# A Mamba round with eight states scaled by ScalarE and folded by accumulating DMAs, and softplus sums moved to accumulating DMAs

## The reference, cut to what matters

```python
ssm = xv @ W_x
dt_raw, Bp, Cp = ssm[..., :8], ssm[..., 8:24], ssm[..., 24:]
delta = softplus(dt_raw @ W_dt + b_dt)
dA = exp(delta[..., None] * A)
dBx = delta[..., None] * Bp[:, :, None, :] * xv[..., None]
h = associative_scan(dA, dBx)          # h[l] = dA[l] * h[l-1] + dBx[l]
y = einsum('bldn,bln->bld', h, Cp) + xv * D
s = y @ W_out
x = x + s * silu(ffn(xn))
```

## Time and profile before

| What | us |
|---|---|
| median of three runs | 855.91 |
| the profiled execution, its own time | 857.77 |
| its span in the trace | 856.0 |
| Mamba rounds, first scan to the end | 406.4 to 856 |
| one round, start of `du` to start of the next | 54.7 to 54.9; 59.75 for the one that begins at 564.96 |
| busy in the span: PE, DVE, ACT, POOL | 680, 673, 485, 502 |

### The profile page before, as it was taken

One profiled execution on the slowest core, in us unless ns is written; L12 is line 12 of the kernel. 1 busy time (PEld: TensorE's weight loads), 2 busy tenths in 40 slices (PEclk: granted clock), 3 DMA queues, 4 the chain that ended last, 5 costly groups with the idle time before them and its releaser, 6 DMA issues. The chain is left out here.

```text
span 856.0 us, 13812 instructions
## 1 busy us (share of the span) xinstructions
PE 679.6 (79%) x4000; PEld 502.5 (59%) x4000; DVE 672.5 (79%) x1203; ACT 484.5 (57%) x946; POOL 501.5 (59%) x289
## 2 busy tenths in 40 slices
PE   1948999997999600376779889898898998989673
PEld 1925555655555400233567777676777876778573
DVE  5856777876656468602799999988999999999994
ACT  1725666565444223245685866946858668586461
POOL 1016510000000177007689999999899999999993
PEclk9968999999999855589899999999999999999998
DMA  8501100010222111022311420413203213142000
...
DMA packets 41608, 55.90 MB, mean 65 GB/s; under 512 B 6601, under 2 KB 31697, under 8 KB 41553
## 3 DMA queue, kind: packets, MB, share of 16 engines
q1 hardware_dynamic: 37776, 50.48, 18.2%
...
## 5 line engine op out<-in xcount | busy, mean ns | idle before, releaser
L1575 DVE TENSOR_TENSOR_SCAN xnT_all<-psum,nfT_all 128x1024 f32<-128x1024 f32 x128 | 285.6, 2273 | 7.9 <-ACT psum L1425 5.2
L1313 PEld LDWEIGHTS psum<-W_out,xnT_all 128*128 128x128 f32 x2048 | 244.1, 197 | 40.0 <-issue 38.0
L1313 PE MATMUL psum<-W_out,xnT_all 128*128 128x128 f32 x2048 | 246.5, 280 | 17.2 <-DVE acc L1591 17.2
L1425 ACT ACTIVATE psum<-delta,A 128x511 f32<-128x511 f32 x256 | 163.2, 678 | 40.7 <-DVE xnT_all L1575 39.9
L1293 POOL TENSOR_TENSOR nfT_all<-nf_all,du 128x1024 f32<-128x1024 f32 x64 | 149.8, 2368 | 7.8 <-DVE xnT_all L1575 7.8
L1293 POOL TENSOR_TENSOR nfT_all<-attn_all,du 128x1024 f32<-128x1024 f32 x64 | 149.3, 2359 | 2.5 <-DVE xnT_all L1575 1.2
L950 POOL COPY pos_w<-pos 128x4 uint32 x8 | 1.8, 222 | 182.8 <-issue 182.8
L1591 DVE SCALAR_TENSOR_TENSOR acc<-psum,Cc,acc 128x128 f32<-128x128 f32 x352 | 96.7, 342 | 7.8 <-PE psum L1313 7.8
L551 POOL DMA_INDIRECT xs_dram<-nf_all,pos x32 | 32.3, 1008 | 66.7 <-issue 55.9
L1313 PE MATMUL psum<-vo_all,wgu 128*128 128x512 f32 (+1 forms) x96 | 49.6, 642 | 26.5 <-DVE hff L1611 24.9
L1313 PE MATMUL psum<-vo_all,W_taps 128*128 (+4 forms) x128 | 60.5, 621 | 1.7 <-DVE psum L1558 1.7
...
## 6 DMA issues: line engine op xcount, KB each, us to landing
attn_all<-bt_dram SPq DMA_DIRECT2D x32, 512.0 KB, 5.4
nf_all<-bt_dram SPq DMA_DIRECT2D x32, 512.0 KB, 3.6
...
```

Source lines behind the costliest of these rows:

```text
L1313: return nc.tensor.matmul(o, l, r, start=start, stop=stop)
L1425: ins = nc.scalar.activation(dA[:, i % RA, k, 1:L], delta[:, p, h, 1:L], ACT.Exp, scale=A[:, h, 2 * q + k:2 * q + k + 1])
L1575: nc.vector.tensor_tensor_scan(hring[:, i % R, :, :].rearrange("p n l -> p (n l)"), dA[:, i % RA, :, :].rearrange("p n l -> p (n l)"), dbx ...
```

## The change

- `ON_ACT` becomes all eight odd states. ACT scales them into eight buffers of `ts`, one in each step: state 2q-1 in steps 1 to 7, state 15 in step 0 of the next round. DVE adds only the eight even states.
- The eight buffers are summed in four folds, written as DMAs that accumulate into their destination (`fold`, issued by POOL): `ts[2:4] += ts[0:2]` in step 7, then, in the next round, `ts[4:6] += ts[2:4]` in step 1, `ts[6:8] += ts[4:6]` in step 3 and `ts[7] += ts[6]` in step 4. The first three move 512 KB, the last 256 KB. Each waits for the fold before it. In the closing round the last three folds are additions on POOL.
- The three softplus sums become accumulating DMAs of 512 KB issued by POOL (`add_to`): `delta += rl`, `e1 += ab`, `delta += e1`. ACT now writes the log straight into `delta`. The third waits until the first two have landed, and `du` and the decays wait until the third has landed.
- `output` moves from step 3 to step 5, behind the issue of `delta += rl`.
- `fa` is gone: `ffn_hidden` works in place in `hff`.

The diff, cut to its core:

```diff
--- before.py
+++ after.py
@@ -1104,7 +1104,7 @@
             NP = NS // 2
             R = 4
             RA = 2
-            ON_ACT = (5, 7, 9, 15)
+            ON_ACT = tuple(range(1, NS, 2))
             ON_DVE = tuple(n for n in range(NS) if n not in ON_ACT)
 
             Bbc = attn_all[:, :, :].rearrange("p j d -> p (j d)").rearrange("p (n l) -> p n l", l=L)
...
-            accP = sb6("accP", [P, TPB, D])
...
+            s_sp = sem("p6_softplus_summed")
+            s_ts = sem("p6_scaled_states_summed")
+            s_last = sem("p6_last_scaled_states_summed")
...
@@ -1216,21 +1216,30 @@
                     def w(n, c):
                         pool.wait_ge(S[n], at(b + 1, n, c))
 
-                    def sum_scaled(c, i):
-
-                        pool.wait_ge(S["ts"], at(c, "ts", i + 1))
-                        pool.wait_ge(S["accP"], at(c, "accP", i if i > 1 else 0))
-                        if i == 1:
-                            pool.wait_ge(S["og"], at(c - 1, "og", 1))
-                        nc.gpsimd.tensor_tensor(accP[:, :, :], ts[:, 0, :, :] if i == 1 else accP[:, :, :],
-                                                ts[:, i, :, :], ALU.add).then_inc(S["accP"], 2 if i == 1 else 1)
+                    def fold(c, k):
+
+                        lo, mid, hi = ((0, 2, 4), (2, 4, 6), (4, 6, 8), (6, 7, 8))[k]
+                        pool.wait_ge(S["ts"], at(c, "ts", hi))
+                        if not scan and k > 1:
+                            pool.wait_ge(s_last, k - 1)
+                        elif k or end:
+                            pool.wait_ge(s_ts, c * 64 + k * 16)
+                        alone(pool)
+                        if scan:
+                            pool.dma_start(ts[:, mid:hi, :, :], ts[:, lo:mid, :, :], accum_op=ALU.add).then_inc(s_ts, 16)
+                        else:
+                            nc.gpsimd.tensor_tensor(ts[:, mid:hi, :, :], ts[:, mid:hi, :, :], ts[:, lo:mid, :, :], ALU.add)\
+                                .then_inc(s_last, 1)
 
                     def output():
 
                         pool.wait_ge(S["acc"], at(b - 1, "acc", len(ON_DVE) * TPB))
-                        pool.wait_ge(S["accP"], at(b - 1, "accP", len(ON_ACT)))
+                        if scan:
+                            pool.wait_ge(s_ts, b * 64)
+                        else:
+                            pool.wait_ge(s_last, 3)
                         pool.wait_ge(s_o, b * 16)
-                        nc.gpsimd.tensor_tensor(ow[:, :, :], acc[:, 1 - p, :, :], accP[:, :, :], ALU.add)\
+                        nc.gpsimd.tensor_tensor(ow[:, :, :], acc[:, 1 - p, :, :], ts[:, 7, :, :], ALU.add)\
                             .then_inc(S["os"], 1)
                         pool.wait_ge(S["os"], at(b - 1, "os", 1))
                         pool.wait_ge(S["G1"], at(b - 1, "G1", 1))
@@ -1241,30 +1250,28 @@
                         nc.gpsimd.tensor_tensor(ow[:, :, :], ow[:, :, :], x_all[:, ds((b - 1) * TPB, TPB), :], ALU.add)\
                             .then_inc(S["ow"], 1)
 
+                    def add_to(total, part):
+                        pool.dma_start(total, part, accum_op=ALU.add).then_inc(s_sp, 16)
+
                     def softplus_high():
-
                         w("lg", 1)
                         w("rl", KH)
-                        w("delta", 0)
                         alone(pool)
-                        nc.gpsimd.tensor_tensor(lg[:, :, :], lg[:, :, :], rl[:, :, :], ALU.add).then_inc(S["sp"], 1)
+                        add_to(delta[:, 1 - p, :, :], rl[:, :, :])
 
                     def softplus_low():
                         w("e1", 1)
-                        nc.gpsimd.tensor_tensor(e1[:, :, :], ab[:, :, :], e1[:, :, :], ALU.add)\
-                            .then_inc(S["corr"], 1)
+                        alone(pool)
+                        add_to(e1[:, :, :], ab[:, :, :])
 
                     def deltas():
-                        w("sp", 1)
-                        w("corr", 1)
-                        pool.wait_ge(S["dA"], at(b, "dA", 0))
-                        pool.wait_ge(S["du"], at(b, "du", 0))
-                        nc.gpsimd.tensor_tensor(delta[:, 1 - p, :, :], e1[:, :, :], lg[:, :, :], ALU.add)\
-                            .then_inc(S["delta"], 1)
+                        pool.wait_ge(s_sp, (b + 1) * 48 + 32)
+                        alone(pool)
+                        add_to(delta[:, 1 - p, :, :], e1[:, :, :])
 
                     def drives():
 
-                        w("delta", 1)
+                        pool.wait_ge(s_sp, (b + 2) * 48)
                         w("xv", KH)
                         pool.wait_ge(S["dbx"], at(b, "dbx", 0))
                         nc.gpsimd.tensor_tensor(du[:, 1 - p, :, :], delta[:, 1 - p, :, :], xv[:, :, :], ALU.mult)\
@@ -1273,19 +1280,19 @@
                     if scan:
                         pool.wait_ge(S["du"], at(b, "du", 1))
                         for q in range(NP):
-                            if q == 1 and end:
-                                sum_scaled(b - 1, 2)
-                            if q == 3 and end:
-                                sum_scaled(b - 1, 3)
-                                output()
-                            if q == 5 and prep:
-                                softplus_high()
+                            if q in (1, 3, 4) and end:
+                                fold(b - 1, (1, 3, 4).index(q) + 1)
+                            if q == 5:
+                                if prep:
+                                    softplus_high()
+                                if end:
+                                    output()
                             if q == 6 and prep:
                                 softplus_low()
                             if q == 7:
                                 if prep:
                                     deltas()
-                                sum_scaled(b, 1)
+                                fold(b, 0)
                             pool.wait_ge(s_bld[q], (b + 1) * 16)
                             for h in range(KH):
                                 i = 2 * q + h
@@ -1301,8 +1308,8 @@
                         deltas()
                         drives()
                     elif end:
-                        sum_scaled(b - 1, 2)
-                        sum_scaled(b - 1, 3)
+                        for k in (1, 2, 3):
+                            fold(b - 1, k)
                         output()
 
                 rounds(pool, round_)
@@ -1417,7 +1424,8 @@
                 def decays(b, p, q):
 
                     if q == 0:
-                        act.wait_ge(S["delta"], at(b, "delta", 1))
+                        act.wait_ge(s_sp, (b + 1) * 48)
+                        alone(act)
                     for h in range(KH):
                         i = 2 * q + h
                         act.wait_ge(S["scan"], at(b, "scan", i + 1 - RA))
@@ -1436,12 +1444,16 @@
                     nc.scalar.activation(bank[bM[h]], bank[bM[h]], ACT.Identity, bias=convb[:, h:h + 1])\
                         .then_inc(S["yh"], 1)
 
-                def scale_state(c, p, i):
+                def scale_state(c, p, i, again):
 
                     n = ON_ACT[i]
                     act.wait_ge(S["G"], at(c, "G", n + 1))
                     act.wait_ge(S["C"], at(c, "C", 1))
-                    act.wait_ge(S["accP"], at(c, "accP", max(i, 1) + 1 - len(ON_ACT)))
+                    if i == 7:
+                        act.wait_ge(S["os"], at(c - 1, "os", 1))
+                    elif again:
+                        act.wait_ge(s_ts, (c - 1) * 64 + (16, 16, 32, 32, 48, 48, 64)[i])
+                        alone(act)
                     for j in range(TPB):
                         ins = nc.scalar.activation(ts[:, i, j, :], bank[Gb[n % 2]][:, j * P:(j + 1) * P], ACT.Copy,
                                                    scale=Cc[:, p, j, n:n + 1])
@@ -1474,9 +1486,9 @@
 
                     def abs_relu(h):
                         w("dt_ps", h + 1)
-                        w("corr", 0)
-                        w("lg", 0)
-                        w("delta", 0)
+                        if scan:
+                            act.wait_ge(s_sp, (b + 1) * 48)
+                            alone(act)
                         nc.scalar.activation(ab[:, h, :], bank[bM[h]], ACT.Abs, bias=b_dt[:, h:h + 1])
                         nc.scalar.activation(rl[:, h, :], bank[bM[h]], ACT.Relu, bias=b_dt[:, h:h + 1])\
                             .then_inc(S["rl"], 1)
@@ -1487,13 +1499,13 @@
 
                     def ln_one_plus():
                         w("ey", 1)
-                        w("delta", 0)
-                        nc.scalar.activation(lg[:, :, :], ab[:, :, :], ACT.Ln, bias=1.0).then_inc(S["lg"], 1)
+                        act.wait_ge(S["du"], at(b, "du", 0))
+                        act.wait_ge(S["dA"], at(b, "dA", 0))
```

(8 more changed lines are left out.)

12 lines of the change are left out of this document (5 added, 7 removed).

## The result

The changed kernel takes **875.12 us** (median of four runs, 871.63 to 875.43) against 856.41 for the kernel before beside it (855.45 to 860.3): ratio 1.020, 95% interval 1.016 to 1.024. Forecast were 852.1, range 843 to 874. The sign was wrong, and the time lies 1.1 us above the range. The profiled execution has a span of 873.6 (own time 875.43) where before it was 856.0.

A forecast was written before the change was run, and what follows sets the result against it. The prediction took a loop through PE, ACT and DVE as the bound: seven rounds at −0.4, back edge −3.0, startup +1.0, round 7 −1.4 and closing +2.4 sum to −3.8, from 855.9 to 852.1 us, range 843 to 874.

The forecast's parts named there:

- The loop PE-ACT-DVE sets the pace: Round's loop through PE, ACT and DVE: 30.0 us of unchanged PE work plus the way back; gains 0.4, to 54.4.
- Busy times: Each engine's work per round: DVE falls to 49.3 us, ACT rises to 43.8, POOL needs 52.6.
- Issues, 1.26 (0.96 to 1.74): POOL's time to issue one DMA, seven added a round: 1.26 us, taken from indirect DMAs.
- issues as the bound: Rival: at 1.74 us an issue POOL needs 56.0 a round and sets the pace, total 866; chance 0.13.
- Landings, 4.2 from the end of the issue: Accumulating DMAs of 512 KB land 4.2 us after their issue ends, bounds 2.7 and 7.0; at 4.2 nothing stalls.
- landings as the bound: Rival: waits along `e1 += ab`, `delta += e1`, `du` in steps 6 and 7 decide from 6.4 us; chance 0.22.
- ACT in steps 6 and 7: "nothing": ACT's added scalings there, 1.05 us each, fall into its waits for PE and cost nothing.
- `output` behind the log: POOL, step 5: waits some 3 us for the log, then 27.7 us to the first dbx, leaving 2.2 slack.
- Startup +1.0: Before the first scan: two issues and two uncovered landings replace two sums, costing 1.0 us.
- Back edge −3.0: Between rounds 2 and 3, where DVE jumps back: PE's wait and slow `ssm` mostly go, saving 3.0 us, bounds 0 and 4.2.
- Round 7, −1.4: Round that prepares nothing: DVE saves 3 us by step 7, but POOL's input comes later, so 1.4 us is gained.
- Closing +2.4: Closing round: one addition behind the last `ts` becomes two, costing 2.4 us.

The follow-up runs named there:

- e6: Changed kernel with SP's store behind the B loads, ACT's next-round decays before step 7's scaling, and in-round B loads filling one partition, not 128: 856.06 us, ratio 0.999.
- e11: Changed kernel with SP's store behind the B loads, ACT's next-round decays before step 7's scaling, and B loads spread one at a time: 860.64 us, ratio 1.003.
- e13: e12 with ACT's scalings of steps 1 and 2 put back where the changed kernel has them: 852.51 us, ratio 0.992.
- e8: Changed kernel with the three softplus sums as additions on POOL again, folds still accumulating DMAs: 867.9 us, ratio 1.012.
- e10: e8 with ACT writing the next round's first decays ahead of the scaling of state 13 in step 7: 863.44 us, ratio 1.004.
- e7: Changed kernel with its accumulating DMAs made plain copies of the same size, the sums left out: 862.31 us, ratio 1.006.
- e2: Changed kernel with ACT writing the next round's step 0 decays ahead of the scaling of state 13 in step 7: 875.41 us, ratio 1.020.
- e4: Kernel before, with its loads of B held back and issued in a bundle, no accumulating DMAs: 858.43 us, ratio 0.999.
- e9: Changed kernel with four states on ACT, their additions on POOL and ACT's order as before; softplus sums still accumulating DMAs: 866.01 us, ratio 1.009.
- e12: Changed kernel: two softplus sums on POOL, output before the first, step 7 decays before scaling, steps 1 and 2 scalings behind exp and log, earlier closing sums: 874.87 us.

## Why the prediction was wrong, point by point

- **The loop PE-ACT-DVE sets the pace, 54.4 a round**: right as a floor. With the waits gone it is 54.6 in three kernels (`e6`, `e11`, `e13`). Against the 54.7 of before the gain is 0.1, not 0.4. The side from `dt` to `ffn_down` fell from 24.7 to 24.0, more than the 0.5 forecast; but "the change takes nothing" from PE's 30.0 was wrong even here. It is 30.6 in `e6`: `dt` lasts 2.4 for 1.9, since its second half waits for the `Cc` that the scaling in step 1 makes late. I had put that at 0.1. (My sum also had a slip: 1.05 less 0.2 is 0.85, not 0.75, and gives 0.3.) In the changed kernel PE's side grew to 32.3.
- **Busy times**: DVE forecast 49.3, measured 49.5; ACT 43.8 and 43.6; POOL 52.6 and 49.4, by the next term.
- **Issues, 1.26 (0.96 to 1.74)**: too high, and outside the bounds. From 694.11 to 720.0 POOL does ten dbx (23.25) and three issues, (25.89 − 23.25)/3 = **0.88** each. The indirect DMAs were a poor neighbour; the rival "issues as the bound" falls.
- **Landings, 4.2 from the end of the issue**: right for one alone (4.40 at startup). Wrong for the one that matters, and here the forecast failed. The upper end of 7.0 was taken from the loads of B *as they lay before*; I moved `output` past SP's queue and costed only POOL's side of it. SP's store and, behind it, every load waited for `output`, and started right where the least covered DMA flies: 9.5. The rival "landings as the bound" had the place and the slack right (2.2 forecast, 2.0 measured). By its own formula, with only the first landing late, 9.5 less the issue's 0.85 gives (8.65 − 4.65) − 2.2 = 1.8 a round over the floor; measured is 56.4 over 54.6. That these agree is partly luck: the measured wait of 4.5 less the slack of 2.0 would be 2.5. (By the formula a round loses 1.25 at a landing of 7.0 and 3.25 at 8.0; I had written 1.15 and 2.75.) The rival was given 0.22, and the range left out its far half.
- **ACT in steps 6 and 7: "nothing"**: the second failed step. The scaling of state 13 stands ahead of the decays of the next step 0. It doesn't fall into a wait, it brings one along (2.27 for PE). Cost alone: 55.9 against 54.6 in the first round (`e8` and `e10`), 1.3, and 1.2 to 1.4 in every later round of `e7`.
- **`output` behind the log**: wait forecast 3, measured 1.9 to 2.1 in four rounds (3.7 in the one with the back edge); 27.7 of chain, 26.2 in `e6` since issues were cheaper. With the sums on POOL, the chain that it stands in is a bound of its own (`e10`).
- **Startup +1.0**: +2.1 by the same stretch here, and +0.6 to +1.2 in the six other kernels with three summed landings there (14.81 in `e2` to 15.49 in `e11`). So the number was right elsewhere, though `e8` and `e10` differ by 2.2 without any landing. Here the last landing took 6.1 from its issue, and why isn't known.
- **Back edge −3.0**: −0.5 by the time of that round. It was 4.4 longer than its neighbours before and is 1.9 longer now, so 2.5 of the extra went, and the slower pace of every round took 1.9 of that back. In `e6` the round is 4.5 shorter than before, beyond the bound of −4.2.
- **Round 7, −1.4**: 0.1 instead. `output` ahead of the dbx of step 5 makes the scans of step 5 wait 2.37 (at 839.03). I had counted the issue and the folds, not that two dbx stood behind it. **Closing +2.4**: +2.5.
- **Not forecast**: the last 1.9 to 2.0. From the end of the last addition to the end of the span it is 2.7 in `before`, `e4`, `e8`, `e9` and `e10` (0, 24 or 29 DMA issues by POOL in the Mamba rounds), 3.3 in `e12` and `e13` (36), and 4.6 in the seven kernels with 53. The trace shows what it is: POOL's closing DRAIN takes 1.38, 3.35, 3.75, 4.32 and 5.71 us with 0, 24, 29, 36 and 53 issues, plain or accumulating (`e7`) alike. That is 0.08 for each issue; up to 29 the store of the output covers it. Why it grows wasn't tried.

The forecast's own span of 852.2 was met by `e6` (851.5), the changed kernel with both orders mended (the store's and ACT's) and without the traffic: what was missing were two places where order makes a wait. That the total fits this well is partly luck: in `e6` a round gains 0.1 for 0.4, the back edge 4.5 for 3.0, and the DRAIN's 2.0 stands in no term.
